# Turning blocks of x ahead of the edge counting, and loading a group's bounds in the middle of the group before

## What is computed

```
edge_index = stack([src, dst])
x = layernorm(x + gat(x, ...8 heads, then 1 head..., edge_index))
x = layernorm(x + gcn(x, ...two layers..., edge_index))
```

## Time and profile before

| | us |
|---|---|
| median of 3 runs | 1778.51 (1774.86 to 1779.06) |
| profiled execution | 1777.28 |
| its span, first to last instruction | 1775.2 |
| TensorE matmuls, busy | 1673.4 (94%) |
| VectorE busy | 1223.8 (69%) |
| ScalarE busy | 798.1 (45%) |
| first counting matmul | 23.8 |
| end of the last group | 79.3 |
| first matmul of the projection | 80.1 |

### The profile page before, as it was taken

How to read it: one execution, slowest core, us unless ns; L and a number is a source line. 1 busy time by engine, 2 the same in 40 slices (tenths; PEclk the granted TensorE clock), 3 DMA queues, 4 the chain that set the end, 5 groups by cost and what they waited for, 6 DMA issues and landing times. The chain is left out here.

```text
span 1775.2 us, 21747 instructions
## 1 busy us (share of the span) xinstructions
PE 1673.4 (94%) x7596; PEld 1393.4 (78%) x7601; DVE 1223.8 (69%) x2336; ACT 798.1 (45%) x1295; POOL 164.7 (9%) x117
## 2 busy tenths in 40 slices
PE   5899999999979999999999899999999975879998
PEld 3588888788857888888888688888888864878898
DVE  8744454654787887788877687888767348974447
ACT  6333321222545565565555455655556225534240
POOL 0023221312200000000000000000000013210003
PEclk9999999999989999999999999999999977989999
DMA  3155575766535765557654765666344321131222
GB/s 135 42 184 184 180 235 167 172 226 205 199 114 197 191 185 148 149 176 213 173 125 173 198 158 160 178 187 168 122 171 182 112 110 36 54 127 55 63 83 105
DMA packets 133808, 268.04 MB, mean 151 GB/s; under 512 B 23738, under 2 KB 83524, under 8 KB 121028
## 3 DMA queue, kind: packets, MB, share of 16 engines
q1 hardware_dynamic: 133700, 266.63, 48.8%
HBM read 206.21 MB, written 60.40 MB: 150 GB/s over the span
## 5 line engine op out<-in xcount | busy, mean ns | idle before, releaser
L41 PE MATMUL bank<-ph,hc 128*128 128x512 f32 x768 | 300.2, 391 | 4.7 <-DMA hc<-h_scratch 3.5
L43 PE MATMUL bank<-ph,hc 128*128 128x512 f32 x768 | 299.5, 390 | 0.0
L42 PE MATMUL bank<-pl,hc 128*128 128x512 f32 x768 | 299.4, 390 | 0.0
L771 DVE CUSTOM_DVE_ANT_0 junk<-bank,a_bc 128x512 bf16<-128x512 f32 (+1 forms) x256 | 129.9, 554 | 195.3 <-ACT st L523 180.1
L41 PE MATMUL bank<-hh,w2h 128*128 128x512 f32 x576 | 226.2, 393 | 14.7 <-DVE w2l L853 10.3
L41 PE MATMUL bank<-wh,xTh 128*128 128x512 f32 x570 | 224.3, 393 | 4.7 <-POOL wl L458 4.7
L43 PE MATMUL bank<-hh,w2l 128*128 128x512 f32 x576 | 225.7, 392 | 0.0
L42 PE MATMUL bank<-hl,w2h 128*128 128x512 f32 x576 | 225.5, 392 | 0.0
L43 PE MATMUL bank<-wh,xTl 128*128 128x512 f32 x570 | 223.3, 392 | 0.0
L42 PE MATMUL bank<-wl,xTh 128*128 128x512 f32 x570 | 223.1, 391 | 0.0
L41 PEld LDWEIGHTS bank<-ph,hc 128*128 128x128 f32 x768 | 144.5, 188 | 36.0 <-DMA hc<-h_scratch 3.9
(11 more groups left out here) (257 smaller groups left out, 2867.6 us busy)
## 6 DMA issues: line engine op xcount, KB each, us to landing
hc<-h_scratch SPq DMA_DIRECT2D x96, 1024.0 KB, 5.4
h_scratch<-st SPq DMA_DIRECT2D x96, 512.0 KB, 3.0
w2r<-in_L_gnn_W SPq DMA_DIRECT2D x96, 384.0 KB, 6.6
wr<-in_L_gnn_W SPq DMA_DIRECT2D x12, 1536.0 KB, 8.7
gwr<-in_L_gnn_W SPq DMA_DIRECT2D x24, 384.0 KB, 3.2
row_bc<-logits_scratch SPq DMA_DIRECT2D x16, 512.0 KB, 13.1
expo_bc<-expo_scratch SPq DMA_DIRECT2D x16, 512.0 KB, 6.2
xr<-in_x SPq DMA_DIRECT2D x2, 1536.0 KB, 8.4
```

Of the source, the lines that this page charges most:

```text
L41: nc.tensor.matmul(out, sh, mh, start=first, stop=False, skip_group_check=not grouped)
L42: nc.tensor.matmul(out, sh, ml, start=False, stop=False, skip_group_check=not grouped)
L43: return nc.tensor.matmul(out, sl, mh, start=False, stop=last, skip_group_check=not grouped)
L771: nc.vector.tensor_tensor_reduce(out=junk[:, s % 2, 0:hi - lo], in0=banks[n % 6][:, lo:hi], in1=a_bc[q % 2][:, k, lo:hi], scale=1.0, scala ...
```

## The change

The registers with a group's bounds are loaded between the firm tiles and the loop of the group before, on VectorE and on TensorE; those of group 0 before the first group. Blocks 0 to 3 of x are turned and made into both parts before the counting, and blocks 4 to 7 are turned and have their high parts made. After group w, TensorE subtracts block w + 4 and turns block w + 8 (while there are such blocks); ScalarE copies the low part of block w + 4 and the high part of block w + 8 in this order. The turning at the start waits no more for `range_done` and `cols_done`; those waits now stand behind it. ScalarE makes the low one-hots of 24 tiles instead of 32, VectorE those of 104 instead of 96.

```diff
-ACT_TILES = 32
+ACT_TILES = 24
...
-    X_BEFORE = 3
+    XA = 4
...
-            for g in range(X_BEFORE):
+            for g in range(XA):
+                x_high(g)
+            act.wait_ge(range_done, 9)
+            for g in range(XA):
+                x_low(g)
+            for g in range(XA, 2 * XA):
                 x_high(g)
...
-                if w < XG:
-                    if w + X_BEFORE < XG:
-                        x_high(w + X_BEFORE)
-                    x_low(w)
+                if w + XA < XG:
+                    x_low(w + XA)
+                if w + 2 * XA < XG:
+                    x_high(w + 2 * XA)
...
+            following = bounds(0)
             for w in range(NW):
-                first = dve.value_load(range_i[w:w + 1, 0:1], min_val=0, max_val=ET - SLOTS)
-                pairs = dve.value_load(range_i[w:w + 1, 1:2], min_val=FIRM // 2 + 1, max_val=EP)
+                first, pairs = following
...
+                if w + 1 < NW:
+                    following = bounds(w + 1)
                 with dve.Fori(FIRM // 2, pairs) as q:
...
-            pe.wait_ge(range_done, 9)
-            pe.wait_ge(cols_done, 3)
             pe.wait_ge(low_out, 1)
             pe.wait_ge(const_c, 4)
-            for g in range(X_BEFORE):
+            for g in range(XA):
                 turn_x(g)
+            for g in range(XA):
+                lessen_x(g)
+            for g in range(XA, 2 * XA):
+                turn_x(g)
+            pe.wait_ge(range_done, 9)
+            following = bounds(0)
+            pe.wait_ge(cols_done, 3)
...
-                first = pe.value_load(range_i[w:w + 1, 0:1], min_val=0, max_val=ET - SLOTS)
-                pairs = pe.value_load(range_i[w:w + 1, 1:2], min_val=FIRM // 2 + 1, max_val=EP)
+                first, pairs = following
...
+                if w + 1 < NW:
+                    following = bounds(w + 1)
                 with pe.Fori(FIRM // 2, pairs) as q:
...
-                if w < XG:
-                    if w + X_BEFORE < XG:
-                        turn_x(w + X_BEFORE)
-                    lessen_x(w)
+                if w + XA < XG:
+                    lessen_x(w + XA)
+                if w + 2 * XA < XG:
+                    turn_x(w + 2 * XA)
```

More of the change, by code:

```diff
@@ L742, in _, with bounds @@
             dve.wait_ge(low_out, 1)
+            def bounds(w):
+                return (dve.value_load(range_i[w:w + 1, 0:1], min_val=0, max_val=ET - SLOTS),
+                        dve.value_load(range_i[w:w + 1, 1:2], min_val=FIRM // 2 + 1, max_val=EP))
+            following = bounds(0)
             for w in range(NW):
-                first = dve.value_load(range_i[w:w + 1, 0:1], min_val=0, max_val=ET - SLOTS)
-                pairs = dve.value_load(range_i[w:w + 1, 1:2], min_val=FIRM // 2 + 1, max_val=EP)
+                first, pairs = following
                 if w >= 2:
@@ L1056, in lessen_x, with bounds @@
                                  start=False, stop=True, skip_group_check=True).then_inc(x_less, 1)
-            pe.wait_ge(range_done, 9)
-            pe.wait_ge(cols_done, 3)
+            def bounds(w):
+                return (pe.value_load(range_i[w:w + 1, 0:1], min_val=0, max_val=ET - SLOTS),
+                        pe.value_load(range_i[w:w + 1, 1:2], min_val=FIRM // 2 + 1, max_val=EP))
             pe.wait_ge(low_out, 1)
             pe.wait_ge(const_c, 4)
-            for g in range(X_BEFORE):
+            for g in range(XA):
                 turn_x(g)
+            for g in range(XA):
[5 more added lines that the diff above has]
+            pe.wait_ge(cols_done, 3)
             pe.wait_ge(low_hot_s, ACT_TILES // TG)
```

## The result

| | before, us | after, us |
|---|---|---|
| median of 22 runs each | 1778.2 (1773.34 to 1781.88) | 1784.2 (1778.61 to 1787.74) |
| ratio | | 1.0031, 95% interval 1.0023 to 1.0040 |
| span of the profiled execution | 1775.2 | 1783.1 |
| first key of VectorE | 21.64 | 22.91 |
| end of group 0's zero matmul | 26.2 | 27.8 |

The change costs 0.31%, about 5.5 us by the ratio. The forecast was 1782.0 us, 4.7 over the profiled execution of before. In the profiled execution of after the stage ends 6.7 later, and the rest of the span is as long as before within 1.2 us (1783.1 - 86.77 = 1696.3 against 1695.1). So the time was lost where the prediction looked for it. TensorE's timeline of after shows how (start us, us, line and operation, count, idle time before it and what ended it); it stands beside the earlier trace rows.

The account below looks back on a forecast made before the run. TensorE's sequencer was taken as the bound; the later start and four stalled steps put group 5 5.3 us late, group 7 4.8 and the stage's end 4.7: 1777.3 + 4.7 = 1782.0 us, range 1776.5 to 1786.5.

Parts of the forecast that it names:

- TensorE's sequencer as the bound: Edge counting: TensorE's instruction issue, not its array, sets the group's 3.39 us, with or without turns.
- Moved loads gain 0: Middle of each group: the two loads' 1.3 us stay in the same sequencer and only move; ordinary groups gain 0.
- The new wait: After groups 0 to 3: TensorE waits 1.18 us for ScalarE's low copy; steps 4.7 us against 3.4.
- The start: Before group 0: first key at 22.8, turns 4 to 7 from about 18.4 to 22, group 0 ends at 27.4.
- Group 5 and after: Group 5 starts at 46.2, 5.3 us late; group 7 at 54.5, 4.8 late; then 3.39 per group.
- the odd pass: Group 5's one extra loop pass: its VectorE key, 43.28 before, was forecast at 49.5 us.
- the sum: Whole counting stage: all steps added up put its end 4.7 us later, giving 1782.0 us.
- First rival, the free sequencer: Turns after groups 0 to 3: a waiting turn leaves the sequencer free; steps 4.46, total 1780.1 us; chance 0.23.
- Second rival, hidden loads: All groups: loads run beside matmul issue, VectorE's keys bound at 3.03 us per group; total 1771.3 us; chance 0.07.
- Third rival, the slow level: Early turns from 18.4: matmuls take 421 ns, group 0 ends 2.9 us later; total 1784.9 us; chance 0.15.
- the cover: Before group 0: turns 4 to 7 finish by about 22, hidden under VectorE's work before its first key at 22.8.

Follow-up runs that it names:

- double_loads: Kernel before with TensorE's two bound loads of each group issued twice; executed once, first projection matmul at 101.9 us against 80.1.
- loads_only: Kernel before with only the bound loads moved to the middle of the preceding group, turns left as they were; ratio to before 0.9996.
- turns_only: Changed kernel with the bound loads put back at each group's start, eight blocks still turned ahead; ratio to before 1.0056.
- seven_ahead: Changed kernel with seven blocks of x turned ahead instead of eight; ratio to before 1.000, first projection matmul at 79.99 us.
- after_again: Changed kernel, unedited, profiled once more; no fall of the clock, first projection matmul at 85.15 us against 80.1 before.
- act_32: Changed kernel with ScalarE making 32 tiles of low one-hots again, VectorE 96; executed once, first projection matmul at 88.0 us against 85.15.
- early_bounds: Changed kernel with seven blocks turned ahead and bounds of groups 6 to 11 loaded before the groups; ratio to before 0.9977.

## Why the prediction was right

It named the cause, the place and nearly the size; point by point:

- **TensorE's sequencer as the bound**: right. `double_loads` shows it, as loads added on TensorE alone lengthen each group by their whole 1.3. The groups without loads (2.60 instead of 3.39) fit, but there VectorE's loads were gone as well, and its keys had become the bound.
- **Moved loads gain 0**: right in the change as a whole (`loads_only`, 0.9996), with an exception that the prediction did not have: behind a blocked turn they save 0.37 a group (`turns_only`).
- **The new wait**: forecast 1.18 of wait and 3.45 from first address calculation to the end of the closing matmul. Measured in group 2: 35.01 - 33.85 = 1.16, and 3.47. The next address calculation came with the release and not 0.1 behind it, so that steps were 4.62 to 4.75 against 4.7. `seven_ahead` takes the wait away, and the loss goes. Group 5's first address calculation came at 46.2 in `after_again`, as forecast.
- **The start**: first key 22.8 forecast, 22.91 measured; turns 4 to 7 from 18.4 in both; end of group 0 at 27.4, measured 27.79 and 27.47 (`after_again`).
- **Group 5 and after**: the key of the odd pass was due at 49.5 and came at 49.60 in `after_again`. The stage ended 5.06 late there instead of 4.7. Most of that lies behind that key: group 7 was to start at 54.5, but its first address calculation came at 54.8. The last key was taken up 2.8 behind 49.6, as in the sum; loads and loop then took 2.4 and not 2.1. The sum gives no row for its 2.1, and the earlier trace rows make it 2.3 (74.4 to 75.4, and 1.3 for the loads). `loads_only` has the same miss, with 0.2 won in groups 5 to 7 instead of 0.5.
- **First rival, the free sequencer**: wrong. The Trainium skill ("Perfetto Trace Analysis", Per-instruction lifecycle) has the sequencer ready as soon as it has pushed; here no address calculation of the next group came before the release (35.0 and 35.01), and in `turns_only` no load (34.6 and 34.55). Its price of 4.46 a step was mis-sized too: from turn to firm tiles the array takes 1.00, not 0.87, and with that it would need 4.6 by itself. Array and sequencer are late together in a stalled group, so the step alone would not have told the two apart; the start of the address calculations did.
- **Second rival, hidden loads**: wrong, by the late groups' 3.4.
- **Third rival, the slow level**: wrong in the place where the prediction put it: the turns from 18.4 took 275 ns each and ended at 22.2. `act_32` shows that the cover can fail, not that the rival's price was right. But the slow level did come, at the turn after group 0, in one of two profiled executions of the changed kernel, at 1.4 us. That is the term that the sum left out. It said that TensorE keeps its fast level through such gaps; the row it used was of the late groups, and at the start of the stage it didn't hold in every execution.

The measured ratio, 1.0031, lies just above the 0.3% that the forecast (0.26%) was just under, and its interval holds both. The prediction gave 0.63 to a change within 0.3% and 0.31 to a slower one, so on which side of that line the result fell was luck. The clean stage accounts for 5.06 of the 5.5 us; how much of the rest is the fall of the clock in some executions can't be told, since unprofiled runs don't show their stages.

Left open: why the clock falls in one execution and not in another. TensorE's idle times ahead of it were the same. No run here separates that.

## What to carry to other kernels

When work is moved so that an engine asks for a buffer, look up in which step of the other engine's queue that buffer comes free: one block fewer ahead (seven instead of eight) turned a request for this group's copy into one for the last group's, and 1.3 us a group into nothing. Here a blocked turn held the whole queue behind it, so count such a wait with everything that the sequencer has yet to issue. Where register loads are the bound, moving them within the loop gives next to nothing; they have to go to a place where the sequencer waits anyway.

## What was unexpected of the hardware

- A turn blocked by a semaphore held the sequencer (next address calculation at 35.0, release at 35.01), but running turns did not: in `early_bounds` the load behind 32 turning matmuls went out at 12.9, when about half of them, which began at 9.85, had been started. In these rows the sequencer ran ahead of an array that was moving, and not past one that was blocked.
- One register load with its checks holds TensorE's sequencer for 0.68 us, although the load itself is recorded with 0.30. In a group of 3.39 the two loads take 1.3, the eight address calculations of the firm tiles 1.1 at a distance of 0.14, and the loop about 0.7.
- The granted clock fell to 0.50 for about 3 us around the first groups in several executions (28.7 to 32.1 in that of after), and in the second one of the same program not at all. Where TensorE had work of its own there it cost 1.4; in `seven_ahead`, whose group 0 took 3.57 for its firm tiles instead of 2.2 but waits for VectorE's keys all the same, it cost nothing that the stage's end shows.
